# Gated cross-attention and a mixture of experts on one core: down products with the weights held still, and transposes moved from TensorE to VectorE and DMA

## What is computed

```python
x = x + tanh(g_xattn) * xattn(layernorm(x), ctx, ctx, wq, wk, wv, wo)      # rope, window of 64, softmax
x = x + tanh(g_ffn)   * ffn(layernorm(x), ...)
# ffn:
up_s   = einsum('th,seh->tse', xt, shared_up)
shared = einsum('tse,she->th', gelu(up_s), shared_down)
probs  = softmax(xt @ router_w.T);  topk_p, topk_i = top_k(probs, 4)
gate   = zeros_like(probs).at[arange, topk_i].add(topk_p)
up_r   = einsum('th,reh->tre', xt, routed_up)
routed = einsum('tre,rhe->th', gelu(up_r) * gate[:, :, None], routed_down)
```

## Time and profile before

| | us |
|---|---|
| median of 3 runs | 533.58 |
| lowest, highest | 531.87, 533.83 |
| the profiled execution | 532.48 |
| its span in the trace | 530.7 |
| TensorE busy, of the span | 514.7 |
| VectorE, ScalarE, GpSimd busy | 344.9, 311.7, 276.0 |

### The profile page before, as it was taken

The page is one execution under the profiler, slowest core; times in us unless marked ns, Lnnn a source line. Parts: engine busy times, 40 slices in busy tenths (PEclk is TensorE's granted clock), DMA queues, the critical chain, the costliest instruction groups (busy, mean ns, idle before and its releaser), DMA issues.

```text
span 530.7 us, 13192 instructions
## 1 busy us (share of the span) xinstructions
PE 514.7 (97%) x4906; PEld 454.2 (86%) x4906; DVE 344.9 (65%) x1121; ACT 311.7 (59%) x861; POOL 276.0 (52%) x213
## 2 busy tenths in 40 slices
PE   9888999999999999999999899999999999999997
PEld 5777797889889988888889789988998999998996
DVE  6868867658675687667766747665656465645444
ACT  3467667475766567665776765664455445644442
POOL 4899998779887978997898325430100010000000
PEclk9999999999999999999999999999999999999999
DMA  7362324011031101220221046206300550045001
GB/s 253 96 173 60 76 59 143 15 36 38 11 105 36 38 1 37 58 55 15 63 57 46 13 156 245 81 1 214 147 1 1 174 186 1 1 142 219 1 1 40
DMA packets 21614, 41.03 MB, mean 77 GB/s; under 512 B 3056, under 2 KB 5360, under 8 KB 21552
## 3 DMA queue, kind: packets, MB, share of 16 engines
q1 hardware_dynamic: 21552, 40.20, 24.6%
HBM read 30.62 MB, written 2.23 MB: 62 GB/s over the span
## 4 chain that ended last, share of the span: by engine, by line
PE 75%; POOL 10%; DVE 6%; issue 5%; ACT 3%; DMA 1%; SPq 0%; DVEq 0%; POOLq 0%; ACTq 0%
PE ring L939 51%; PE psS L939 9%; PE psO L1140 5%; PE psS L1109 4%; PE psT L1121 4%; POOL arena L433 3%; POOL arena L435 2%; POOL prob L439 2%; DVE arena L724 1%; POOL wl L447 1%; POOL arena L426 1%; PE psT L1086 1%; DMA craw<-in_ctx 1%; ACT prob L585 1%; POOL arena L423 1%
## 5 line engine op out<-in xcount | busy, mean ns | idle before, releaser
L939 PE MATMUL ring<-xTh,wh 128*128 128x512 f32 x272 | 111.3, 409 | 1.6 <-DVE wl L795 1.4
L939 PE MATMUL ring<-xTl,wh 128*128 128x512 f32 x272 | 106.9, 393 | 0.0
L939 PE MATMUL ring<-xTh,wl 128*128 128x512 f32 x272 | 106.8, 393 | 0.0
L939 PE MATMUL ring<-wh,oTh 128*128 128x256 f32 x272 | 78.3, 288 | 2.0 <-POOL wl L447 0.8
L939 PE MATMUL ring<-wh,oTl 128*128 128x256 f32 x272 | 76.6, 282 | 0.0
L939 PE MATMUL ring<-wl,oTh 128*128 128x256 f32 x272 | 76.4, 281 | 0.0
L439 POOL TENSOR_TENSOR prob<-prob,rinv 128x512 f32<-128x512 f32 x64 | 68.1, 1065 | 15.1 <-DVE rinv L853 15.0
L782 DVE TENSOR_TENSOR oTl<-prob,oTh 128x512 fp32r<-128x512 f32 x64 | 45.5, 710 | 43.5 <-ACT oTh L531 43.3
L531 ACT ACTIVATE oTh<-prob 128x512 fp32r<-128x512 f32 x64 | 40.4, 631 | 55.6 <-PE ring L939 25.2
L774 DVE TENSOR_TENSOR prob<-sneg,arena 128x512 f32<-128x512 f32 x64 | 47.4, 741 | 26.4 <-ACT sneg L515 26.4
L515 ACT ACTIVATE sneg<-ring 128x512 f32<-128x512 f32 x72 | 42.9, 596 | 36.7 <-PE ring L939 36.2
(11 more groups left out here) (118 smaller groups left out, 1247.9 us busy)
## 6 DMA issues: line engine op xcount, KB each, us to landing
arena<-gate_scratch SPq DMA_DIRECT2D x64, 256.0 KB, 6.3
raw<-in_e SPq DMA_DIRECT2D x18, 256.0 KB, 2.6
raw<-in_w SPq DMA_DIRECT2D x16, 256.0 KB, 3.4
arena<-arena SPq DMA_DIRECT2D x16, 256.0 KB, 3.1
arena<-arena SPq DMA_DIRECT2D x16, 192.0 KB, 3.5
out<-x SPq DMA_DIRECT2D x16, 128.0 KB, 6.0
x<-in_x SPq DMA_DIRECT2D x3, 512.0 KB, 4.1
craw<-in_ctx SPq DMA_DIRECT2D x3, 512.0 KB, 5.5
```

The source lines that it names most:

```text
L939: last = pe.matmul(out, a, b, start=start and i == 0 and j == 0, stop=stop and i == n - 1 and j == 2, skip_group_check=check)
```

## The change

**Down products.** The down weights become the stationary operand (128 columns of `wh` or `wl`) and the activations move past in 512 columns: 2 feature blocks by 3 parts, 6 products of 512 columns. The sums are now by features, so `z` needs x by features too, and the result leaves in that layout.

**x and normalised x** (batches 1 to 3, and x of all 4 for `z`). VectorE turns 32 by 32 blocks in one instruction over 1024 columns (`turn` from `xn`, `back` from x), and SyncE issues 16 DMAs of 32 partitions x 8 x 32 elements each, SBUF to SBUF, which put the blocks in place (`move`). One run of a transfer is 128 bytes. There are seven sets of these, 3 for `turn` and 4 for `back`, 112 DMAs in all. The buffers are those of `pT`, which the attention no longer needs then. The first turning, `("xT", B)`, stays on TensorE.

**Router and gates.** The router products take the 32 columns of router weights as the stationary operand and move 512 tokens: 4 products instead of 16. Four block transposes on VectorE turn the logits, and four turn the gates; TensorE's gate transposes go.

**Slots.** `stat` 3, both normalisations 4, `turn` 5, `xhi` (rounding, ScalarE) 9, `xlo` (rest, VectorE) 10, `r` 11, `rexp` 12, `pick_a` 13, `pick_b` 14, `gT` 15, `back` 11. Gelu of expert n waits for the gate product of n - 2 and no longer for its rest, and gated activations rotate through four buffers. At the end of the attention stage several steps of ScalarE, VectorE and TensorE stand in another order.

```diff
@@ slots
-            for e, kind in ((4, "stat"), (6, "norm_a"), (7, "norm_b"), (9, "xT"), (10, "r"), (11, "rexp"),
-                            (12, "pick_a"), (13, "pick_b"), (15, "gT")):
+            for e, kind in ((3, "stat"), (4, "norm_a"), (4, "norm_b")):
+                after[b * NE + e].append((kind, B + b + 1))
+            for e, kind in ((5, "turn"), (9, "xhi"), (10, "xlo"), (11, "r"), (12, "rexp"), (13, "pick_a"),
+                            (14, "pick_b"), (15, "gT")):
+                after[b * NE + e].append((kind, b + 1))
         for b in range(B):
+            after[b * NE + 11].append(("back", b))
@@ sync
+            def move(dst, blocks, done):
+                for a in range(4):
+                    mine = blocks[QUAD * a:QUAD * (a + 1), :].rearrange("p (m c j) -> p m c j", m=KC * TT, c=4)
+                    for c in range(4):
+                        to = dst[QUAD * c:QUAD * (c + 1), :].rearrange("p (m a j) -> p m a j", m=KC * TT, a=4)
+                        sp.dma_start(to[:, :, a, :], mine[:, :, c, :]).then_inc(done, 16)
@@ scalar
-                if n >= 2:
+                if n >= 2 and experts[n - 2][1] < NS:
                     act.wait_ge(f_lo, n - 1)
+                elif n >= 2:
+                    b, e = experts[n - 2]
+                    act.wait_ge(f_mul, b * NR + e - NS + 1)
+                elif kind == "xhi":
+                    X = side(B + n)
+                    act.wait_ge(xn_moved, 256 * n)
...
+                    act.activation(xTh[X][:, :, :], xnT, ACT.Copy).then_inc(xT_hi, 1)
@@ scalar, end of the attention
+                if c == CLOSING - 1:
+                    copy_transposed(58)
                 softmax_numerator(c)
...
-            copy_transposed(58)
+            copy_transposed(59)
             softmax_numerator(61)
-            copy_transposed(59)
+            round_att(29)
             do(("rexp", 0))
@@ vector
+                elif kind == "turn":
+                    dve.wait_ge(ln_norm, B + n + 1)
...
+                    dve.transpose(xn_blocks.rearrange("p (k t d) -> p k t d", k=KC, t=TT),
+                                  xn[:, :, :].rearrange("p t (k d) -> p k t d", k=KC)).then_inc(xn_turned, 1)
+                elif kind == "back":
...
+                    dve.transpose(x1_blocks.rearrange("p (k t d) -> p k t d", k=KC, t=TT),
+                                  x[:, n, :, :].rearrange("p t (k d) -> p k t d", k=KC)).then_inc(x1_turned, 1)
@@ tensor
-                for t in range(TT):
-                    half, at = t // 2, (t % 2) * D
-                    last = product(sums(b, half)[:, at:at + D],
-                                   [(hi[:, t * P:(t + 1) * P], lo[:, t * P:(t + 1) * P])],
-                                   [cols(i, D, D)], start=(e == 0 and t % 2 == 0), stop=(e == NE - 1),
-                                   check=True)
-                    last.then_inc(down_pe, 1)
+                for kc in range(KC):
+                    product(sums(b, kc), [cols(i, D + kc * P, P)], [gated_parts(n)], start=e == 0,
+                            stop=e == NE - 1, check=True).then_inc(down_pe, 1)
```

More of the change, by code:

```diff
@@ L369, in store @@
             def store(b):
-                for t in range(TT):
-                    sp.wait_ge(z_out, TT * b + t + 1)
-                    sp.dma_start(out_d[b][:, t, :], x[:, b, t, :]).then_inc(out_done, 16)
+                for i in range(4):
+                    part = slice(i % 2 * (L // 2), (i % 2 + 1) * (L // 2))
+                    sp.wait_ge(z_out, 4 * b + i + 1)
+                    sp.dma_start(out_d[b][:, i // 2, part], z_of(b)[:, i // 2, part]).then_inc(out_done, 16)
             def do(job):
@@ L731, in router @@
             def router(b):
-                job = ("r", b)
-                by_parts = banks(job)[0][:, 0:2 * TT * NR].rearrange("p (t a e) -> p t a e", t=TT, a=2)
                 dve.wait_ge(r_pe, b + 1)
-                link(dve.tensor_copy(lex[:, :, :], by_parts[:, :, 0, :]))
-                link(dve.tensor_tensor(lex[:, :, :], lex[:, :, :], by_parts[:, :, 1, :], ALU.add))
+                if b == 0:
+                    dve.wait_ge(c_lo, KC + B - 1)
+                    dve.memset(gate[:, :, :], 0.0)
+                by_tokens = banks(("r", b))[0][0:QUAD, :].rearrange("p (t a j) -> p t a j", t=TT, a=4)
+                for a in range(4):
+                    last = dve.transpose(logits[QUAD * a:QUAD * (a + 1), :, :], by_tokens[:, :, a, :])
+                link(last)
+                link(dve.tensor_tensor(lex[:, :, :], logits[:, :, 0:NR], logits[:, :, NR:], ALU.add))
                 link(dve.tensor_reduce(lmax[:, :], lex[:, :, :], AX_X, ALU.max))
@@ L901, in _ @@
                 for job in jobs:
+                    if (c, job[0]) == (CLOSING - 2, "xT"):
+                        invert(CLOSING - 2)
                     do(job)
@@ L1081, in do @@
                     X = side(B + n)
-                    for t in range(TT):
-                        for kc in range(KC):
-                            for part in (xTh[X], xTl[X]):
-                                last = pe.matmul(two[0][:, t * 2 * NR:(t + 1) * 2 * NR],
-                                                 part[:, kc, t * P:(t + 1) * P],
-                                                 rw_parts[:, kc, :, :].rearrange("p a e -> p (a e)"),
-                                                 start=kc == 0 and part is xTh[X],
-                                                 stop=kc == KC - 1 and part is xTl[X])
-                    last.then_inc(r_pe, 1)
-                elif kind == "gT":
-                    pe.wait_ge(r_gate, n + 1)
-                    for t in range(TT):
-                        last = pe.transpose(two[0][0:NR, t * P:(t + 1) * P], gate[:, t, :], ident[:, :])
-                    last.then_inc(gT_pe, 1)
+                    for kc in range(KC):
+                        for part in (xTh[X], xTl[X]):
+                            last = pe.matmul(two[0][0:2 * NR, :], rw_parts[:, kc, :, :].rearrange("p a e -> p (a e)"),
+                                             part[:, kc, :], start=kc == 0 and part is xTh[X],
+                                             stop=kc == KC - 1 and part is xTl[X])
+                    last.then_inc(r_pe, 1)
             def scores(c):
@@ L1180, in _ @@
             expert(0)
+            transpose_probs(61)
             do(("y", UNITS - 2))
-            do(("gT", 0))
-            transpose_probs(61)
-            expert(1)
             values(30)
             transpose_probs(62)
+            expert(1)
+            transpose_probs(63)
             expert(2)
-            transpose_probs(63)
+            values(31)
             down(0)
-            values(31)
             expert(3)
```

137 lines of the change are left out of this document (79 added, 58 removed).

## The result

| us | before | after |
|---|---|---|
| median | 533.58 | 534.96 |
| lowest to highest | 531.87 to 534.58 | 533.33 to 536.66 |
| runs | 21 | 21 |
| the profiled execution | 532.48 | 533.67 |
| its span | 530.7 | 531.9 |

The ratio of after to before is 1.0024, with a 95% interval from 1.0014 to 1.0033. So the change costs 0.24%, which is less than the 0.5% that a single comparison can tell. TensorE, which bound the kernel, nevertheless lost work: it is busy 7.7 us less than in the earlier trace rows (the page of after: span, then busy time of each engine).

What follows compares the result with a forecast made beforehand. TensorE was taken to bound the kernel: from 532.5 us, 11.1 us of gains and charges of 0.5, 0.9, 2.85 and 0.5 gave 526.2, forecast as 526.0 us, range 521 to 538.

Steps and rivals of the forecast that it cites:

- TensorE bounds the expert stage: Expert stage: a queue of TensorE work, so work leaving TensorE shortens the program while other engines stay ahead.
- The gains, 11.1 us: Down products 2.9, turning x 2.6, router 2.3, gate transposes 1.3, end of attention 2.0 us, if nothing waits.
- the end of the attention: Router, gate and reordering savings there, 2.0 us taken, between 0.5 and 3, since part hangs on ScalarE's softmax.
- Slot 4: Statistics one slot before normalisation: ScalarE stands still, down(4) stops 0.3 us in each of three batches.
- The chain of VectorE in batch 0: Batch 0: `back` behind the router's steps uses up most slack; 0.5 us charged, 0 to 1.5.
- The moves: Sixteen DMAs after `turn`, 0.50 us apart, landing 3.1 us: TensorE stops 0.95 us per batch, 2.85 us.
- The prediction's own formula: Stop per batch at `xhi`: SyncE's start 4.05, plus 15 issue spacings, plus landing, minus the 13.7 us limit.
- the weight load: Batch 0: load ahead of the moves on SyncE, waiting for GpSimd's rest of that piece; another 0.5 us.
- The other weight loads queue behind the moves by 8 us, with 11 to spare: SyncE's queue: these loads are delayed 8 us by the moves, with 4 slots (11 us) to spare.
- The bytes and the runs of 128 bytes are no term: Moves: 512 KB is hidden behind 8 us of issuing, and short runs show no cost of their own.
- rival B: SyncE issues the moves slower, 531 to 545 us; chance 0.10 up to its even point, 0.18 beyond.
- even point: Rival B's issue spacing, 0.63 us, at which the changed kernel takes as long as before.

Runs made afterwards that it cites:

- c_after: The changed kernel itself, unaltered, run again on the same chip beside the kernel with eight unused products added: 534.88 us, ratio 1.0027.

## Why the prediction was wrong

It said 526.0 us and faster; the kernel is at 534.96, within the range of 521 to 538 and on the other side of before. Each step against its measurement:

- **TensorE bounds the expert stage: right.** What left TensorE without a wait in its place shortened the program, by 9.4 us without the moves.
- **The gains, 11.1 us: right.** Without moves the profiled execution is 524.13 us against 532.48, 8.4 us. TensorE's stops in it (1.45, 0.49, 0.40, 0.36, 0.33, 0.18, 0.18) sum to 3.4 us, where before had 0.5 of them. So 8.4 + 2.9 = 11.3 us were gained. Term by term: the down products 0.039 us per expert and 2.8 us in all (2.9 forecast), of which only 1.6 showed in the net; turning x 2.9 (2.6); a router piece 0.92 us where TensorE doesn't wait for `xTl` (0.93), so 0.77 each as forecast; the end of the attention about 2.6 at the same point of the first experts (2.0). The Trainium skill's rule (TensorE: Matmul & The Clock Gate, on how a matmul executes, step 3), which the prediction weighed, gives equal time for equal columns; the trace of after differs from it by these 0.039 us per expert.
- **Slot 4: too small in batch 0.** 0.3 us were forecast in each batch, and it is 1.46 in batch 0, where GpSimd also makes weights, and 0.17 and 0.18 in the others. Sum 1.8 against 0.9.
- **The chain of VectorE in batch 0: about right in kind, too small.** 0.5 us were charged; stops of 0.36, 0.36 and 0.47 us are there beside those named, 1.2 us.
- **The moves: the step that failed, by the size of one input.** 0.95 us in each batch and 0.5 more in batch 0 made 3.35 us. From `z` to `z`, after against the kernel without moves, they cost 4.5, 2.3 and 2.7 us, 9.5 in the traces and 10.7 in the medians. (The profiled execution of after, 533.67 us, is 1.3 below its median; its clock fell only where that costs nothing.) The issues came 0.653 us apart instead of 0.50, which is 15 x 0.153 = 2.3 us per batch, and the landing took 2.0 us instead of 3.1, which gives 1.1 back. The prediction's own formula with these two values gives 4.05 + 9.8 + 2.0 - 13.7 = 2.15 us per batch, against 2.3 and 2.7 measured in batches 1 and 2. There the formula was right, and its input was not.
- **The moves in batch 0: a second stop that had no term.** The stop in slot 9 is 2.31 us there, 0.6 above that of batch 1 and about what was charged for the weight load (0.5). Behind it TensorE waits once more, for `xTl`: 1.26 us in `c_after`, against 0.16 in the other batches. VectorE's subtraction took 2.32 us there and 1.22 in the others. In the kernel without moves it took as long (2.33), and TensorE did not wait for it. So the 2.2 us that batch 0 costs above batch 1 are mostly these two, and not the clock.
- **"The other weight loads queue behind the moves by 8 us, with 11 to spare": wrong once the moves are hidden.** With sixteen moves ahead of them they are late by 10.5 us, and in the kernel with `xhi` a slot later ScalarE waits for one of them.
- **The bytes and the runs of 128 bytes are no term: right**, by the kernel with longer runs and by that with four moves.

So the kernel took the path of rival B. The prediction put its even point at 0.63 us between issues, named that as the figure that would make it wrong, and held it for unlikely because it was "above every row shown". That was a misreading. The 0.58 us between the two copies inside SBUF are one issue of 0.53 and the gap behind it; the second copy's own issue lasts 0.58, and with such a gap of 0.05 its spacing is 0.63. The trace of before has sixteen issues of this line (least/median/most in ns):

```profile
L331 SPq DMA_DIRECT2D arena<-arena x16: 583/597/897, 18.1 to 289.8; - x16
```

A median of 0.60 us and the gap make 0.64, close to the 0.653 that came. With 0.64 and the landing forecast of 3.1 us the stop would have been 4.05 + 9.6 + 3.1 - 13.7 = 3.05 us per batch, and the sum 532.5 us, no change. That this comes nearer to the result than the formula with the measured inputs (529.8) is luck: the landing was forecast 1.1 us too long, and the second stop of batch 0 was missing.

## What to carry to other kernels

A transpose that goes over DMA is priced by the issues on its one queue: count them, take their spacing (the issue and the gap behind it) from the row of the same kind of copy, and work out when the last one lands; bytes and landing come after. When a chain has a few us of limit, the slot in which it starts and the slot in which it is used are worth more than the chain itself: here a slot at each end made 1.9% out of a loss of 0.2%. And what is queued behind a burst on the same queue (weight loads here) needs its own due time checked after the repair, since the next wait appears there.

## What the runs showed of the hardware

- A DMA from SyncE's queue that copies 32 KB between 32 partitions of SBUF took 0.61 us to issue as 8 runs of 128 bytes per partition, 0.65 us from one to the next, and 0.59 us as one run of 1 KB. Over 128 partitions with 8 runs it took 0.68 us (median of 28) for four times the bytes. Plain loads on the same queue took 0.43 us.
- Behind a stop TensorE's granted clock fell from 1.00 to 0.50, from 2.4 to 1.2 GHz, for some 3.5 us, in which it does 1.7 us less work. It fell behind stops of 2.31 us (after, batch 0), 2.16 (`c_after`, batch 2), 1.94 (longer runs, batch 2) and 1.91 (old end of the attention). It did not fall behind stops of 2.38 us (`c_after`, batch 0), 2.07 (after, batch 2) and 1.72 (after, batch 1, and the kernel with added products, batch 2). The length of the stop alone does not decide it. What the fall costs depends on the place: 0.1 us in batch 0 of after, where VectorE sets the pace behind the stop, and 1.2 us in batch 2 of `c_after`. It makes executions of one kernel differ: with the longer runs the four with a mean clock of 0.997 took 533.6 to 534.1 us, the six with 0.999 or 1.000 took 532.1 to 533.4.
- A block transpose of 128 x 1024 fp32 took VectorE 1.24 us, in the prediction's range. The subtraction `xTl` took 1.22 us alone and 2.32 us in batch 0, where GpSimd works beside VectorE.
